# Dense attention of a two-layer decoder: side work moved to other places within a head's time, rows fetched every second head

## The chip, the cores and the metric

One core of a Trainium2 chip runs the whole program. The metric is the device time of one execution in microseconds. The kernel is timed several times; the median stands for it. One further execution is profiled, and that one has its own time.

## The reference, cut to what matters

Two layers: latent attention, a cross attention and a mixture of experts, then dense attention, a sigmoid mix and a quantised feed-forward. The change touches the dense attention stage and the side work done under it. In the reference's terms:

```python
# end of the first layer: x gets the four weighted expert rows of each token
routed = zeros_like(x).at[tok].add(out_slots * flat_w[order][:, None])
x = x + ...                                   # residual, then the next layer
# dense attention (2 batches of 512 in one pass over 8 pairs of heads, twice)
q, k, v = einsum('bpd,hde->bphe', layernorm(x), W_Q / W_K / W_V) + b
attn = softmax(where(causal, q @ k / sqrt(128), IGNORE))
x = x + einsum('bqhe,hed->bqd', attn @ v, W_O) + b_O
# mix with a sigmoid of the context, per token and channel
x = x + 0.6 * sigmoid(si + sj + b) + 0.4 * layernorm(x)
# ternary weights of the feed-forward
scale = 1 / mean(abs(w));  wq = clip(round(w * scale), -1, 1) / scale
```

The token stream `X` has 16 tiles of 128 tokens by 512. Batches 0 and 1 are tiles 0 to 7, batches 2 and 3 are tiles 8 to 15.

## The kernel before, in words

The dense stage is one loop over 64 **slots**, `for i in range(NI + 2)`, written out once per engine. A slot computes the scores and the softmax of head turn i, transposes the probabilities of turn i-1 and multiplies them with V, and projects Q, K and V of turn i+1. In an odd slot the output projection of the last pair of heads comes on top. `DenseOrder.steps(i)` (L1559) gives the order within a slot, and all engines follow it: scores 0 and 1, project Q, transpose 0, project K, scores 2, transpose 1, scores 3, transpose 2, project V, in odd slots four outputs, and then the values. Engines run in order and meet at semaphores.

In this text a time "at 7.84" counts from the start of its slot on PE (the first L1761 matmul of score 0). All matmuls are done in three parts (high and low halves of both operands), so each drained PSUM bank is read twice: ACT copies the high part, and DVE then subtracts to get the low part. For one slot that gives a chain between PE, ACT and DVE:

- Q projection: ACT `d_qk` L1884, DVE `d_qk` L2019, then DVE `d_rv` L2035 (reciprocals for rows 0 and 1 of the softmax); POOL L2217 scales those two rows of P.
- transpose 0: ACT `d_PTh` L1899, DVE `d_PTl` L2042.
- K projection: ACT L1884, DVE L2019. Then DVE `d_mx` L2027 and `d_nb` L2029 of score 2, ACT exponential L1892, ACT L1899 and DVE L2042 of transpose 1, DVE L2027 of score 3, ACT L1892, ACT L1899 and DVE L2042 of transpose 2. The values on PE (L1805 to L1807) wait for that last L2042.
- V projection: ACT `d_Vh` L1878, DVE `d_Vl` L2013. In an odd slot the four outputs are then added to X by DVE, L2048; PE's third output waits for the first of these additions.
- values: ACT `d_zh` L1906, DVE `d_zl` L2053, at the start of the next slot.

In every fourth slot (i = 2, 6, 10, ...; called **splitting slots** here, all of them even) the next pair's weights are split: ACT L1859 after each of the three projections, and POOL L2191, a subtraction of two SBUF tiles: two of them follow POOL's first two L2217, the third follows its last two. SP loads weights one slot after (L1608, L1613).

The **side work** before the change:

- *Additions of later tiles.* Tiles 8 to 15 still lack their four expert rows. POOL fetches the rows with indirect DMAs into `d_cmb` (`fetch`, L2179, four a tile), one tile a slot in slots 18 to 25. DVE adds one tile a slot in slots 20 to 27 (`combine`, L1985): row 0 after project Q, row 1 after project K, row 2 after transpose 1, row 3 after transpose 2, and statistics (`stats`) after project V.
- *Weight sums.* 24 pieces of 128x1024 are loaded by SP into three buffers; ACT sums their absolute values (`absum`, L1910), two a slot in slots 33 to 44, after project Q and project V.
- *Rounding.* In slots 47 to 58 the 24 pieces are loaded again; DVE scales and clips each (`rounded`, L2073 and L2075), after project Q and project V; ACT subtracts a constant and writes bf16 (`settle`, L1916), after project K and project V; SP stores it.
- *Mixing.* Tiles 0 to 7 get the sigmoid mix: DVE takes statistics again (`retake`, after project V in slots 32 to 39), POOL turns them into factors (`weigh`, slots 35 and 39), DVE scales the tile (L2062, after transpose 1 in slot 36+t), ACT computes the tanh (`lean`, L1928, after transpose 2) and DVE adds it (L2066, after project Q of the next slot).

Of the kernel before, what the change touches and what calls it, by code (L numbers as in the profile page):

```python
# [1508 lines left out]
NPC = 24  # L1509


class DenseOrder:
# [22 lines left out]
    def tiles(self, i):  # L1535

        return {0: ((), (4, 5, 6, 7)), 29: ((8,), (9,)), 30: ((10,), (11,)), 31: ((12,), (13,)), 32: ((14,), (15,))}.get(i, ((), ()))

    def sums(self, i):

        return [2 * (i - 33), 2 * (i - 33) + 1] if 33 <= i < 45 else []

    def rounds(self, i):

        return [2 * (i - 47), 2 * (i - 47) + 1] if 47 <= i < 59 else []

    def mixed(self, i):

        return i - 36 if 36 <= i < 44 else -1

    def side(self, i):

# [41 lines left out]
DENSE = DenseOrder()  # L1594
# [78 lines left out]
def dense_sp(e, S, a, M, W, G, wscr):  # L1673
    def weights(ws):
        e.wait_ge(S["d_wl"], 3 * ws)
        dense_load(e, a, W, G, ws)

    def weights_o(ws):
        e.wait_ge(S["d_wol"], ws)
        dense_load_o(e, a, W, G, ws)  # L1680

    def piece(m):
        n = m % NPC
        if 3 <= m < NPC + 3:
            e.wait_ge(S["d_abs"], m - 2)
        elif m >= NPC + 3:
            e.wait_ge(S["d_set"], n - 2)
        dst = M.piece[m % 3] if n < 16 else M.piece[m % 3].rearrange("p (k n) -> p k n", k=2)
        e.dma_start(dst, dense_piece(a, n)).then_inc(S[f"d_pc{m % 3}"], 16)

    def store(n):
        e.wait_ge(S["d_set"], n + 1)
        e.dma_start(wscr[n // 8, :, n % 8 * 1024:n % 8 * 1024 + 1024], M.tern[n % 2]).then_inc(S[f"d_st{n % 2}"], 16)

    for ws in range(1, 8):
        weights(ws)
        weights_o(ws)
    weights(8)
    e.dma_start(M.wi[:, :], a["wiT"]).then_inc(S["d_ctx"], 16)
    e.dma_start(M.bb[:, :], a["L1_xattn_b"].partition_broadcast(128)).then_inc(S["d_ctx"], 16)  # L1700
    e.wait_ge(S["d_cb"], 16)
    e.dma_start(M.cT[:, :, :], a["ctxT"][0:2].rearrange("b p n -> p b n")).then_inc(S["d_ctx"], 16)
    for m in range(3):
        piece(m)
    for i in range(30, 62):
        if i % 4 == 3:
            if i < 56:
                weights((i + 5) // 4)
            weights_o((i + 1) // 4)
        for n in DENSE.sums(i):  # L1710
            piece(n + 3)
        for n in DENSE.rounds(i):
            store(n)
            if n + 3 < NPC:
                piece(NPC + n + 3)
    for r in range(2):
        e.wait_ge(S[f"d_st{r}"], 16 * (NPC // 2))
# [133 lines left out]
def dense_act(e, S, M, W, G):  # L1851
    ps, O = G.ps, DENSE
# [55 lines left out]
    def absum(n):  # L1908
        e.wait_ge(S[f"d_pc{n % 3}"], 16 * (n // 3 + 1))
        e.activation(M.piece[n % 3], M.piece[n % 3], ACT.Abs, accum_out=M.ws[:, n // 8, n % 8:n % 8 + 1]).then_inc(S["d_abs"], 1)  # L1910

    def settle(n):
        e.wait_ge(S["d_rnd"], n + 1)
        if n >= 2:
            e.wait_ge(S[f"d_st{n % 2}"], 16 * (n // 2))
        e.activation(M.tern[n % 2], M.piece[n % 3], ACT.Copy, bias=-MAGIC).then_inc(S["d_set"], 1)  # L1916
# [7 lines left out]
    def lean(t):  # L1924
        e.wait_ge(S["d_b7"], 2 + t // 4)
        if t:
            e.wait_ge(S["d_mixed"], t)
        e.activation(M.sg, M.row, ACT.Tanh, bias=M.si[:, t:t + 1], scale=0.5).then_inc(S["d_sg"], 1)  # L1928
# [12 lines left out]
    for i in range(NI + 2):  # L1941
        if i % 4 == 2 and 6 <= i < NI:
            split_o((i - 2) // 4)
        for s in O.steps(i):
            if s[0] == "s":
                soft(i, s[1])
            elif s[0] == "p":
                project(s[1], s[2])
                if i % 4 == 2 and i + 2 < NI:
                    split_w((i + 2) // 4, "qkv".index(s[1]))  # L1950
                if s[1] in "qv" and O.sums(i):
                    absum(O.sums(i)[s[1] == "v"])
                if s[1] in "kv" and O.rounds(i):
                    settle(O.rounds(i)[s[1] == "v"])
            elif s[0] == "x":
                turn_x(s[1])
            elif s[0] == "b":
                if s[1] in ("m0", "m1"):
                    row(int(s[1][1]))
            elif s[0] == "t":  # L1960
                turn_p(i - 1, s[1])
                if s[1] == 2 and O.mixed(i) >= 0:
                    lean(O.mixed(i))
            elif s[0] == "z":
                values(i - 1)


def dense_dve(e, S, M, W, G):
# [22 lines left out]
    def stats(t):  # L1991
        e.wait_ge(S["d_cb"], t + 1)
        ln_stats_dve(e, S, dv, G, range(t, t + 1))
# [61 lines left out]
    def retake(t):  # L2055
        e.wait_ge(S["d_xa"], 60 if t < 4 else 64)
        ln_stats_dve(e, S, dv, G, range(t, t + 1))
# [53 lines left out]
    combine(5)  # L2111
    project("k", 0)
    for i in range(NI + 2):
        adding = i - 12 if 20 <= i < 28 else -1
        for s in O.steps(i):
            if s[0] == "s":
                peak(i, s[1])
            elif s[0] == "p":
                project(s[1], s[2])
                if s[1] == "q":  # L2120
                    invert(i, 0)
                    invert(i, 1)
                    if 29 <= i <= 32:
                        norm(2 * i - 50)
                        norm(2 * i - 49)
                if adding >= 0:
                    if s[1] == "v":
                        stats(adding)
                    else:
                        combine(adding, ("qk".index(s[1]),))  # L2130
                if s[1] == "q" and O.mixed(i - 1) >= 0:
                    mix(O.mixed(i - 1), 1)
                if s[1] == "q" and i == 45:
                    e.wait_ge(S["d_abs"], NPC)
                    e.tensor_reduce(G.wsc[:, :, 0], M.ws[:, :, :], AX.X, ALU.add).then_inc(S["d_wsum"], 1)
                if s[1] == "v" and 32 <= i < 40:
                    retake(i - 32)
                if s[1] in "qv" and O.rounds(i):
                    rounded(O.rounds(i)[s[1] == "v"])
                if i == 0 and s[1] == "q":  # L2140
                    stats(5)
                if i == 0 and s[1] == "k":
                    combine(7)
            elif s[0] == "x":
                turn_x(s[1])
                if i == 0 and s[1] < 6:
                    norm(s[1] + 2)
            elif s[0] == "b":
                side(s[1])
            elif s[0] == "t":  # L2150
                turn_p(i - 1, s[1])
                if s[1] == 1 and O.mixed(i) >= 0:
                    mix(O.mixed(i), 0)
                if adding >= 0 and s[1] >= 1:
                    combine(adding, (s[1] + 1,))
            elif s[0] == "o":
                output(s[1], s[2])
            else:
                values(i - 1)
            if i == 0 and s == ("s", 1):  # L2160
                stats(4)
                combine(6)
            if i == 0 and s == ("s", 3):
                for t in (6, 7):
                    stats(t)
                norm(4)
                norm(5)
            if i < NI and s == (("t", 2) if i else ("s", 3)):
                if i + 1 == NI:
                    invert(i, 0)  # L2170
                    invert(i, 1)
                invert(i, 2)
                invert(i, 3)


def dense_pool(e, S, M, W, G, eoscr):
# [52 lines left out]
    for i in range(NI):  # L2229
        if i % 4 == 2 and i >= 6:  # L2230
            split_o((i - 2) // 4)
        norm(i, 0)
        norm(i, 1)
        if i == 0:
            for t in (5, 6, 7):
                rstd(t)
        if i % 4 == 2 and i + 2 < NI:
            split_w((i + 2) // 4, 0)
            split_w((i + 2) // 4, 1)
        norm(i, 2)  # L2240
        norm(i, 3)
        if i % 4 == 2 and i + 2 < NI:
            split_w((i + 2) // 4, 2)
        if i < 2:
            for t in range(4 * i, 4 * i + 4):
                bias(t)
        if 18 <= i < 26:
            fetch(i - 10)
        if i == 27:
            ln_rstd_pool(e, S, G, range(8, 12), 12)  # L2250
        if i == 28:
            ln_rstd_pool(e, S, G, range(12, 16), 16)
        if 29 <= i <= 32:
            bias(2 * i - 50)
            bias(2 * i - 49)
        if i in (35, 39):
            weigh((i - 35) // 4)
# [567 lines left out]
```

## Time and profile before

| what | value |
|---|---|
| median of 3 runs | 3533.98 us (3522.2 to 3544.41) |
| profiled execution, its time | 3511.81 us |
| its span, first to last instruction | 3510.5 us |
| mean granted TensorE clock | 0.955 |
| busy: PE, DVE, ACT, POOL | 89%, 55%, 44%, 38% of the span |
| chain that ended last: PE, DVE, ACT, issue | 56%, 16%, 7%, 6% of the span |
| dense stage loop | about 1945 to 3108 us of the span |

A window row of the trace gives the length of a stretch, each engine's busy time with its number of instructions, and the mean granted TensorE clock (1.00 is the upper level). A timeline row gives start, duration, engine, line, operation, output<-inputs, and in brackets how long the engine sat idle before it and who released it. Starts and ends of neighbours overlap by up to 0.1 us, because instructions are pipelined. PE is busy 89% on average, but the stage has quiet slots and disturbed ones, and only the rows by slot show the difference.

### The profile page before, as it was taken

How to read it: one execution, taken by the hardware profiler on the slowest of the kernel's cores; microseconds unless marked ns; L12 is line 12 of the kernel's file. 1: busy time of each engine (PE TensorE's matmuls, PEld its weight loads, DVE VectorE, ACT ScalarE, POOL GpSimd, SP SyncE). 2: the span in 40 equal slices, each digit the busy share in tenths (PEclk: the TensorE clock that was granted, in tenths of full speed). 3: DMA queues.
4: the chain of work that ended last, by engine and by line, in shares of the span. 5: the costliest groups of instructions: out<-in, count | busy, mean ns of one | idle time of the engine just before them, and what ended most of it. 6: DMA issues, size and time to landing. Idle time of an engine off the chain costs nothing.

```text
span 3510.5 us, 47291 instructions
## 1 busy us (share of the span) xinstructions
PE 3135.9 (89%) x17554; PEld 2141.0 (61%) x17587; DVE 1935.9 (55%) x3349; ACT 1541.3 (44%) x2738; POOL 1349.2 (38%) x1271
## 2 busy tenths in 40 slices
PE   7899886899897789999995899988999999988898
PEld 3344432433333458888884788877887877855565
DVE  3454444677775634444444544455555556557776
ACT  1222221577776324444442344433455544435554
POOL 2324232333321655665664533454434444310000
PEclk9899898799998899999997899999999999999999
DMA  3000000000002125665665101122022233020000
GB/s 116 1 1 1 1 1 7 6 1 1 1 1 71 37 88 189 198 201 189 199 199 164 49 25 30 49 78 85 25 85 79 85 109 109 30 78 7 13 13 19
DMA packets 148007, 231.56 MB, mean 66 GB/s; under 512 B 12314, under 2 KB 70511, under 8 KB 147524
## 3 DMA queue, kind: packets, MB, share of 16 engines
q1 hardware_dynamic: 130372, 178.15, 15.7%
q0 software_dynamic: 17408, 50.38, 4.9%
q8 instruction: 142, 2.33, 0.3%
q14 instruction: 85, 0.70, 0.1%
HBM read 180.16 MB, written 48.33 MB: 65 GB/s over the span
## 4 chain that ended last, share of the span: by engine, by line
PE 56%; DVE 16%; ACT 7%; issue 6%; POOL 1%; DMA 1%; SPq 0%; POOLq 0%; ACTq 0%; DVEq 0%; another core or an unknown queue 0%
PE ps L1370 10%; PE ps L1372 9%; PE ps L1371 9%; PE ps L829 3%; PE ps L840 3%; PE ps L797 2%; PE ps L2395 2%; DVE d_PTl L2042 2%; DVE d_mx L2027 2%; PE ps L1090 2%; PE ps L2425 2%; PE ps L2414 1%; ACT d_PTh L1899 1%; DVE d_qk L2019 1%; ACT d_qk L1884 1%
## 5 line engine op out<-in xcount | busy, mean ns | idle before, releaser
L2217 POOL TENSOR_SCALAR d_P<-d_P,d_rv 128x128 f32<-128x128 f32 (+3 forms) x256 | 302.2, 1191 | 548.6 <-DVE d_rv L2035 548.3
L937 DVE TENSOR_REDUCE b_mx<-ps 128x2 f32<-128x1024 f32 x256 | 312.4, 1224 | 115.9 <-PE ps L818 114.1
L904 ACT ACTIVATE b_PT<-ps 128x512 f32<-128x512 f32 x512 | 278.5, 600 | 62.3 <-PE ps L829 58.2
L1492 POOL TENSOR_TENSOR x_wl<-x_wr,x_wh 128x1024 fp32r<-128x1024 f32 x96 | 227.5, 2401 | 185.6 <-ACT x_wh L1416 185.5
L1892 ACT ACTIVATE d_P<-ps,d_nb 128x128 f32<-128x128 f32 (+3 forms) x256 | 135.1, 528 | 253.4 <-DVE d_nb L2029 249.4
L829 PE MATMUL ps<-b_Q,b_KT 64*128 64x512 f32 x512 | 208.3, 469 | 19.6 <-ACT b_PT L904 19.5
L1370 PE MATMUL ps<-d_xh,d_wh 128*128 128x512 f32 x512 | 215.7, 421 | 1.4 <-DVE d_xl L2004 1.4
L818 PE MATMUL ps<-b_KT,b_Q 64*128 64x512 f32 x512 | 205.1, 482 | 4.0 <-DVE b_mx L937 3.1
L1372 PE MATMUL ps<-d_xh,d_wl 128*128 128x512 f32 x512 | 204.1, 399 | 0.0
L2042 DVE TENSOR_TENSOR d_PTl<-ps,d_PTh 128x384 fp32r<-128x384 f32 (+1 forms) x192 | 114.9, 599 | 159.7 <-ACT d_PTh L1899 159.3
L1371 PE MATMUL ps<-d_xl,d_wh 128*128 128x512 f32 x512 | 202.2, 395 | 0.0
L1370 PE MATMUL ps<-x_XH,x_wh 128*128 128x512 f32 x512 | 199.6, 390 | 1.4 <-DVE x_XL L1456 1.4
L1372 PE MATMUL ps<-x_XH,x_wl 128*128 128x512 f32 x512 | 199.7, 390 | 0.0
L1371 PE MATMUL ps<-x_XL,x_wh 128*128 128x512 f32 x512 | 199.5, 390 | 0.0
L462 ACT ACTIVATE a_P<-ps 128x2048 f32<-128x2048 f32 (+1 forms) x48 | 76.4, 1593 | 215.8 <-PE ps L326 194.3
L1464 DVE TENSOR_TENSOR x_ag<-ps,x_sg 128x512 f32<-128x512 f32 x64 | 44.3, 692 | 217.0 <-PE ps L1372 217.0
L1483 POOL DMA_INDIRECT x_Xe<-hscr,x_TI x128 | 139.7, 1092 | 59.1 <-issue 29.7
L829 PEld LDWEIGHTS ps<-b_Q,b_KT 64*128 64x128 f32 x512 | 84.6, 187 | 124.7 <-ACT b_PT L904 88.4
L1370 PE MATMUL ps<-d_wh,d_xh 128*128 128x256 f32 x512 | 151.1, 295 | 1.4 <-DVE d_xl L2004 1.4
L1370 PE MATMUL ps<-d_woh,d_zh 128*128 128x512 f32 x256 | 110.0, 430 | 41.7 <-DVE X L2048 37.0
L1372 PE MATMUL ps<-d_wh,d_xl 128*128 128x256 f32 x512 | 145.8, 285 | 0.0
L1371 PE MATMUL ps<-d_wl,d_xh 128*128 128x256 f32 x512 | 145.8, 285 | 0.0
(378 smaller groups left out, 8383.9 us busy)
## 6 DMA issues: line engine op xcount, KB each, us to landing
x_wr<-in_L_ffn_w SPq DMA_DIRECT2D x32, 1024.0 KB, 7.9
eoscr<-x_eo SPq DMA_DIRECT2D x32, 1024.0 KB, 5.4
x_wr<-in_L_ffn_w SPq DMA_DIRECT2D x32, 512.0 KB, 8.6
d_w<-in_L_attn_W_Q SPq DMA_DIRECT2D x32, 256.0 KB, 3.3
d_w<-in_L_attn_W_K SPq DMA_DIRECT2D x32, 256.0 KB, 4.5
d_w<-in_L_attn_W_V SPq DMA_DIRECT2D x32, 256.0 KB, 5.3
d_wo<-in_L_attn_W_O SPq DMA_DIRECT2D x16, 512.0 KB, 5.6
d_cmb<-in_wgT SPq DMA_DIRECT2D x16, 512.0 KB, 3.9
```

The lines of the kernel that those rows point to most:

```text
L818: e.matmul(ps[:, 2 * (t % 2) + h, :], M.Q1[rows, r % 4, q * 128:q * 128 + 128], M.KT[rows, b % 2, g, :], start=True, stop=True).then_inc(S ...
L829: e.matmul(ps[:, 4 + y, :], M.KT[rows, b % 2, g, k * 128:k * 128 + 128], M.Q2[rows, (2 * j + p) % 4, :], start=True, stop=True).then_inc(S ...
L904: e.activation(M.PT[:, half, v % 2, 2 * p + y, :], ps[:, 4 + y, :], ACT.Exp, scale=0.25).then_inc(S["b_ex"], 1)
L937: e.tensor_reduce(M.mx[:, r % 2, q, :], ps[:, 2 * (t % 2):2 * (t % 2) + 2, :], AX.X, ALU.max).then_inc(S["b_mx"], 1)
L1370: e.matmul(out, lh, rh, start=j == 0, stop=False)
L1371: e.matmul(out, lh, rl, start=False, stop=False)
L1372: t = e.matmul(out, ll, rh, start=False, stop=j == n - 1)
L1483: e.indirect_dma_start(out=M.Xe[:, z, s, :], out_offset=None, in_=hscr, in_offset=bass.IndirectOffsetOnAxis(ap=W.TI[:, 4 * x + s:4 * x + s ...
L1492: e.tensor_tensor(M.wl[:, z, k:k + 2, :], W.wr[:, z, k:k + 2, :], M.wh[:, z, k:k + 2, :].bitcast(F32), ALU.subtract).then_inc(S["x_wl"], 1)
L1892: e.activation(M.P[:, y, POFF[q]:POFF[q] + w], ps[:, q % 2, 0:w], ACT.Exp, bias=M.nb[:, y, q:q + 1], scale=SCALE, accum_out=M.sm[:, y, q:q ...
L2042: e.tensor_tensor(M.PTl[:, c0:c0 + n], ps[:, 2 + c % 2, 0:n], M.PTh[:, c0:c0 + n].bitcast(F32), ALU.subtract).then_inc(S["d_tl"], 1)
L2217: e.tensor_scalar(P, P, M.rv[:, y, q:q + 1], None, ALU.mult).then_inc(S["d_nm"], 1)
```

## The change

It moves the side work; nothing is computed differently. Positions are those of `steps(i)`.

- Additions: tiles 8 to 15 are added in slots 12 to 27, one tile in two slots: rows 0 and 1 after transpose 0 of the even slot, row 2 after transpose 0 of the odd slot, row 3 and the statistics after the last output. Fetches are issued in slots 10, 12, ..., 24.
- Sums and rounding: `pieces(i, first)` gives three pieces to an odd slot and one to an even slot. `absum`: one after transpose 0, in odd slots two more after project V. `rounded`: one after transpose 0, in odd slots two more after the last output. `settle`: one after project V, in even slots two more (those rounded after the outputs) after transpose 0. SP's order of loads and stores stays as it was.
- Mixing: one slot later (slots 37 to 45). DVE's addition and the next tile's scaling stand together after transpose 0, the tanh after project K, and two `retake` after the last output of slots 33, 35, 37 and 39.

```diff
+    def pieces(self, i, first):
+        n = 2 * (i - first)
+        if not 0 <= n < NPC:
+            return [], []
+        return ([n], [n + 1, n + 2]) if i % 2 else ([n + 1], [])
+
     def sums(self, i):
-        return [2 * (i - 33), 2 * (i - 33) + 1] if 33 <= i < 45 else []
+        return self.pieces(i, 33)
     def rounds(self, i):
-        return [2 * (i - 47), 2 * (i - 47) + 1] if 47 <= i < 59 else []
+        return self.pieces(i, 47)
     def mixed(self, i):
-        return i - 36 if 36 <= i < 44 else -1
+        return i - 37 if 37 <= i < 45 else -1
+    def added(self, i):
+        return 8 + (i - 12) // 2 if 12 <= i < 28 else -1
...
 # dense_act
-                if s[1] in "qv" and O.sums(i):
-                    absum(O.sums(i)[s[1] == "v"])
-                if s[1] in "kv" and O.rounds(i):
-                    settle(O.rounds(i)[s[1] == "v"])
+                if s[1] == "k" and O.mixed(i) >= 0:
+                    lean(O.mixed(i))
+                if s[1] == "v":
+                    for n in O.sums(i)[1]:
+                        absum(n)
+                    for n in O.rounds(i)[0]:
+                        settle(n)
...
                 turn_p(i - 1, s[1])
-                if s[1] == 2 and O.mixed(i) >= 0:
-                    lean(O.mixed(i))
+                if s[1] == 0:
+                    for n in O.sums(i)[0]:
+                        absum(n)
+                    for n in O.rounds(i - 1)[1]:
+                        settle(n)
...
 # dense_dve
-        adding = i - 12 if 20 <= i < 28 else -1
...
-                if adding >= 0:
-                    if s[1] == "v":
-                        stats(adding)
-                    else:
-                        combine(adding, ("qk".index(s[1]),))
-                if s[1] == "q" and O.mixed(i - 1) >= 0:
-                    mix(O.mixed(i - 1), 1)
...
-                if s[1] == "v" and 32 <= i < 40:
-                    retake(i - 32)
-                if s[1] in "qv" and O.rounds(i):
-                    rounded(O.rounds(i)[s[1] == "v"])
...
                 turn_p(i - 1, s[1])
-                if s[1] == 1 and O.mixed(i) >= 0:
-                    mix(O.mixed(i), 0)
-                if adding >= 0 and s[1] >= 1:
-                    combine(adding, (s[1] + 1,))
+                if s[1] == 0:
+                    if O.added(i) >= 0:
+                        combine(O.added(i), (2,) if i % 2 else (0, 1))
+                    if O.mixed(i - 1) >= 0:
+                        mix(O.mixed(i - 1), 1)
+                    if O.mixed(i) >= 0:
+                        mix(O.mixed(i), 0)
+                    for n in O.rounds(i)[0]:
+                        rounded(n)
             elif s[0] == "o":
                 output(s[1], s[2])
+                if s[2] == 3:
+                    if O.added(i) >= 0:
+                        combine(O.added(i), (3,))
+                        stats(O.added(i))
+                    if 33 <= i < 40:
+                        retake(i - 33)
+                        retake(i - 32)
+                    for n in O.rounds(i)[1]:
+                        rounded(n)
...
 # dense_pool, after the slot's own work
-        if 18 <= i < 26:
-            fetch(i - 10)
+        if 10 <= i < 26 and i % 2 == 0:
+            fetch((i + 6) // 2)
```

## Rows read from the trace of the kernel before

**Rows 1.** Windows: quiet even slot 10, odd slot 11; slots 20-27; 33-43; 47-58.

```profile
2118.79:2133.15 14.36, 14.02 (x89) 11.95 (x87) 7.12 (x19) 10.05 (x19) 9.39 (x6) 1.00 0.13 37
2133.15:2152.78 19.63, 19.50 (x112) 16.44 (x111) 9.68 (x23) 6.27 (x15) 8.75 (x7) 1.00 0.29 81
2288.82:2453.46 164.64, 143.23 (x786) 119.89 (x785) 97.65 (x224) 57.76 (x128) 82.53 (x67) 0.94 0.27 82
2540.81:2745.58 204.77, 192.03 (x1112) 162.19 (x1111) 113.54 (x275) 108.58 (x231) 86.97 (x70) 0.99 0.28 88
2794.24:3018.15 223.91, 207.05 (x1179) 174.23 (x1177) 132.98 (x299) 108.78 (x215) 99.70 (x61) 0.98 0.34 105
```

**Rows 2.** Window of slot 34, with eight small matmuls of the mix on PE.

```profile
2561.48:2577.02 15.54, 15.54 (x104) 13.80 (x103) 8.24 (x22) 11.23 (x22) 9.48 (x6) 1.00 0.11 35
```

**Rows 3.** Timeline of PE in slot 22, which starts at 2329.91: its stall.

```profile
2346.02 0.58 PE L1805 MATMUL ps<-d_PTh,d_Vh 128*128 128x256 f32 x1 [2.44 <-DVE d_PTl L2042]
```

**Rows 4.** Timeline of DVE in quiet slot 16, which starts at 2220.78.

```profile
2221.70 0.75 DVE L2053 SCALAR_TENSOR_TENSOR d_zl<-ps,d_bv,d_zh 128x512 fp32r<-128x512 f32 x1 [1.89 <-ACT d_zh L1906]
...
2228.62 0.75 DVE L2019 SCALAR_TENSOR_TENSOR d_qk<-ps,d_bk,d_qk 128x512 fp32r<-128x512 f32 x1 [1.71 <-ACT d_qk L1884]
```

**Rows 5.** Timeline of ACT in slot 16, and the tile view of `d_cmb`.

```profile
2227.90 0.69 ACT L1884 ACTIVATE d_qk<-ps,d_bk 128x512 fp32r<-128x512 f32 x1 [2.01 <-PE ps L1372]
...
L1916 ACT ACTIVATE d_cmb<-d_cmb x24: 1042/1057/1058, 2801.9 to 3019.6; 128x1024 bf16<-128x1024 f32 x24
...
DMA to landing us min/median/max: 2.0/3.7/8.1
```

**Rows 6.** Timeline of DVE and POOL in quiet splitting slot 14, which starts at 2186.78.

```profile
2194.62 0.75 DVE L2019 SCALAR_TENSOR_TENSOR d_qk<-ps,d_bk,d_qk 128x512 fp32r<-128x512 f32 x1 [1.06 <-ACT d_qk L1884]
...
2192.35 1.50 POOL L2217 TENSOR_SCALAR d_P<-d_P,d_rv 128x128 f32<-128x128 f32 x2 [1.22 <-DVE d_rv L2035]
2193.82 4.79 POOL L2191 TENSOR_TENSOR d_wl<-d_w,d_wh 128x1024 fp32r<-128x1024 f32 x2
```

**Rows 7.** Timeline of DVE and POOL in slot 22, the splitting slot with additions.

```profile
2335.36 0.73 DVE L1985 SCALAR_TENSOR_TENSOR X<-d_cmb,Wt,X 128x512 f32<-128x512 f32 x1
2338.41 1.99 DVE L1985 SCALAR_TENSOR_TENSOR X<-d_cmb,Wt,X 128x512 f32<-128x512 f32 x1
...
2337.44 5.24 POOL L2191 TENSOR_TENSOR d_wl<-d_w,d_wh 128x1024 fp32r<-128x1024 f32 x2
```

**Rows 8.** Timeline of DVE and POOL in splitting slot 38; L2062's line view.

```profile
2639.73 0.67 DVE L2066 SCALAR_TENSOR_TENSOR X<-d_xn,X 128x512 f32<-128x512 f32 x1
2645.11 1.70 DVE L2062 TENSOR_SCALAR X<-X,d_ab 128x512 f32<-128x512 f32 x1
...
2641.74 4.79 POOL L2191 TENSOR_TENSOR d_wl<-d_w,d_wh 128x1024 fp32r<-128x1024 f32 x2
...
L2062 DVE TENSOR_SCALAR X<-X,d_ab x8: 536/537/1711, 2608.6 to 2735.8; 128x512 f32<-128x512 f32 x8
```

**Rows 9.** Timeline of DVE in slot 49: one piece rounded after project V.

```profile
2844.88 0.74 DVE L2073 TENSOR_SCALAR d_cmb<-d_cmb,wsc 128x1024 f32<-128x1024 f32 x1
2845.66 0.87 DVE L2075 TENSOR_SCALAR d_cmb<-d_cmb 128x1024 f32<-128x1024 f32 x1
```

**Rows 10.** Timeline of DVE and POOL in slot 21: an addition beside POOL's L2217.

```profile
2313.00 0.84 DVE L1985 SCALAR_TENSOR_TENSOR X<-d_cmb,Wt,X 128x512 f32<-128x512 f32 x1
...
2312.22 1.51 POOL L2217 TENSOR_SCALAR d_P<-d_P,d_rv 128x128 f32<-128x128 f32 x2
```

**Rows 11.** Windows of slots 21, 22, 26 and 49: clock and PE time.

```profile
2304.49:2329.91 25.42, 22.18 (x112) 18.37 (x111) 14.67 (x34) 6.27 (x15) 14.80 (x14) 0.87 0.29 82
2329.91:2347.47 17.56, 14.91 (x88) 12.50 (x87) 11.03 (x24) 10.06 (x19) 10.30 (x6) 0.94 0.11 32
2412.29:2429.21 16.92, 14.28 (x89) 11.87 (x87) 10.40 (x23) 10.06 (x19) 9.67 (x6) 1.00 0.17 47
2829.79:2853.48 23.69, 21.25 (x112) 17.66 (x111) 13.81 (x29) 9.23 (x18) 8.82 (x6) 0.93 0.32 100
```

More of the change, by code:

```diff
@@ L1709, in dense_sp @@
             weights_o((i + 1) // 4)
-        for n in DENSE.sums(i):
+        for n in sum(DENSE.sums(i), []):
             piece(n + 3)
-        for n in DENSE.rounds(i):
+        for n in sum(DENSE.rounds(i), []):
             store(n)
```

## The prediction, made before the changed kernel was run

> **What bounds the kernel now.** I read the windows slot by slot first, because PE's 89% hides two kinds of slot. A quiet even slot takes 14.36 us with 14.02 of PE work, a quiet odd one 19.63 with 19.50 [rows 1]: PE sets the pace and nothing moved elsewhere can shorten them. The three stretches with side work are longer. A quiet pair is 33.99. Slots 20 to 27 take 164.64, against 4 x 33.99 = 135.96: 28.7 too much. Slots 33 to 43 (six odd, five even, 189.58 when quiet) take 204.77: 15.2 too much. Slots 47 to 58 take 223.91 against 203.94: 20.0 too much. Together **63.8 us**, the most this change can give back.
>
> Then the waits. In slot 22 PE stands 2.44 us before the values, for DVE's L2042 of transpose 2 [rows 3]. That instruction ends a chain that begins with the K projection: DVE L2019, peak, exponential, transposes 1 and 2, each waiting for the other engine. Whatever is queued on DVE after project K, transpose 1 or transpose 2 lengthens it one for one. Before DVE's L2019 of K there is a hole: after transpose 0 DVE idles 1.71 us [rows 4], ACT 2.01 [rows 5]. Another is at the end of an odd slot, 1.89 before L2053 [rows 4]. In a splitting slot ACT's weight split delays transpose 0, and DVE's hole is 1.06 [rows 6].
>
> A delay costs PE speed as well. PE's busy time in slot 22 is 14.91 instead of 14.02 at a mean clock of 0.94, in slot 49 21.25 instead of 19.50 at 0.93, while slot 26 keeps 1.00 [rows 1, 11]. So a stall of this size sometimes drops the clock to its lower level of 1.2 GHz for a while, at about 1.75 us a time.
>
> **The change part by part.** *Additions.* One row takes 0.73 [rows 7], the next starts 0.05 later because it waits for it. In slots 12, 16, 20, 24 two rows start near 6.1 and end near 7.6; L2019 is due at 7.84: nothing, covered by the 1.71 hole. In odd slots one row fits there. Row 3 and the statistics (0.73 and about 1.1, the latter an estimate from a row of the same width and two tiny instructions) just fill the 1.89. So outside the splitting slots the 28.7 us disappear. The cover gone, a row would cost its 0.75.
>
> In splitting slots 14, 18, 22, 26 DVE is free at 6.78. Row 0 runs to 7.43. POOL's two L2217 end at 5.57 + 1.50 = 7.07 and the weight subtraction L2191 is due at 7.04 [rows 6]. Row 1 can only issue at 7.47. What happens to it is in slot 22: a row that started 0.97 us after L2191 took 1.99 instead of 0.73, and ended 0.56 after the first L2191's 2.40 (half of 4.79) were over [rows 6, 7]. The pair took 5.24 instead of 4.79, so POOL waited in turn. I take it so here: L2191 gets in when row 0 is through (7.3), ends at 9.7, row 1 ends at 10.3, L2019 starts at 10.2 instead of 7.84. Cost 2.3 a slot, 9.2 in all. Bounds: no collision, rows end at 8.25, 0.4 a slot; both halves of the split in front, 4.8.
>
> *Fetches.* They stay at four a tile, now behind POOL's last L2217 of even slots; in splitting slots also behind the third L2191. POOL's first two L2217 of the next odd slot then run later, but PE needs only all four, and the last two wait for reciprocals at the slot's end: nothing. The landing takes 3.7 us, 8.1 at most [rows 5]; a tile's buffer was freed at the end of the odd slot before, and some 15 us are left until its rows are due. The wait of `fetch` is met when reached.
>
> *Sums.* ACT's pieces (1.06 us by the like-sized L1916 [rows 5]) fit in the 2.01 hole after transpose 0, and two after project V in odd slots lie before the outputs, where ACT has nothing to do. Zero; in slots 34, 38, 42 as now, the same instructions in another order between Q's and K's L1884.
>
> *Mixing.* In quiet slots addition (0.67) and scaling (0.54) end near 7.3 [rows 8]: zero. Two `retake` need 2.1 of 1.89; L2053 slips 0.2, which the softmax of scores 0 and 1 absorbs. In slots 38 and 42 the scaling L2062 comes after L2066, at 7.3, when L2191 has begun. Slot 38 shows the price: 1.70 instead of 0.54, ending 0.28 after the pair of L2191 [rows 8]. Now it is the first of the two: end at 10.0, L2019 at 9.9, 2.0 a slot, 4.0 in all; at best 0, at worst 4.5. The small matmuls of slot 34 stay, 15.54 - 14.36 = 1.2 [rows 1, 2]; slots 36 and 40 have fewer, I take 0.5 each (between 0 and 1.2). 2.2 in all.
>
> *Rounding.* L2073 and L2075 take 0.74 and up to 0.87 [rows 9]: 6.05 to 7.7, before 7.84, in all odd slots and in 48, 52, 56: zero, with 0.1 to spare. Two pieces after the outputs take 3.1 of 1.89: L2053 slips 0.9 to 1.2, ACT's Q drain perhaps 0.1. In slots 50, 54, 58 L2075 waits for L2073 and meets L2191 as row 1 does, 0.1 later: 2.4 a slot, 7.2 in all. If it did not collide, ACT would decide: weight split and two `settle` (2 x 1.0) before K's L1884, which starts 0.85 late. At worst 4.9. The `settle` after project V then waits for L2075, and ACT's L1906 of the next slot slips; ACT has slack there. SP's order is unchanged; stores and reloads have a slot's time or most of one, against 8.1 for the longest landing [rows 5].
>
> *Clock.* Nine stalls of 2.0 to 2.4 more. One of the two alike (slots 22, 26) came with a low clock [rows 11]; I take half, 9 x 0.5 x 1.75 = 7.9, with 0 and 15.8 as bounds.
>
> Sum: 9.2 + 4.0 + 7.2 + 2.2 + 7.9 = 30.5 left of 63.8, **gain 33.3**. The profiled execution's 3511.8 becomes 3478.5. The median of the runs is 22 us above it; I take the gain from it: 3534.0 - 33.3 = **3501**.
>
> Beside a collision there is a weaker contact: in slot 21 an addition started while POOL's second L2217 ran and took 0.84, not 0.73, and ended only 0.11 after it [rows 10]. I price such contacts at 0.1, inside the slack. The Trainium skill, SBUF — State Buffer, section "Who interferes with whom", says that a DVE instruction with two SBUF inputs, or in a two-port mode, and a GpSimd one that reads SBUF take the shared port pair in turn, whoever starts first for its whole instruction. For L2191 the trace agrees (1.99 for 0.73). For L2217 it does not (0.84); by the rule that row would have waited to the end of L2217.
>
> **Rivals.** (a) *The later DVE instruction gets in ahead of the split.* Against it: it issues 0.4 us after L2191 is due; for it: L2062 has no wait before it and follows L2066 directly. Left over: 4 x 0.4 + 3 x 0.85 + 2.2 = 6.4; gain 57.4, 3477.
>
> (b) *Waits of whole instructions also for L2217.* The first DVE instruction in the hole would wait for POOL's first L2217 (to about 6.3), the second for the next; L2019 comes 0.6 late in the 13 quiet slots with two instructions (four of additions, nine of rounding): 8 more, gain 25, 3509. Rows 10 speak against it. This is the rule that the Trainium skill's page states, worked out here from rows.
>
> (c) *Slower: the DVE instruction waits behind both L2191*, in slots 14 to 58 with splits, until 12.1; L2019 is 4.8 late (4.5 in slots 38 and 42), 42.6 in nine slots. Stalls that long go with a clock like slot 21's, 22.18 of PE instead of 19.50 [rows 1, 11], 2.7 each, 24.1. With 2.2 that leaves 69, 5 more than now: 3539. It decides from 61.6 / 9 = 6.8 us a slot. Against it: in slot 22 the row got in between the two L2191 [rows 7].
>
> (d) *A transfer comes late*, a fetched tile or a reloaded piece: it decides from 15 us of landing, against 8.1; 15 us lost over the stage give 3516.
>
> **Chances.** Forecast 0.60, (a) 0.20, (b) 0.08, (c) 0.05, (d) 0.07. The forecast's own range, by the clock's bounds, is 3493 to 3509. With (a) below and (b) and the runs' scatter of 11 above, the range is 3470 to 3520. One per cent, 35 us, is about what a measurement can tell: (a) lies beyond it, and some four tenths of the forecast, where few stalls cost clock. Faster by over 1%: 0.46; within: 0.50; slower: 0.04.
>
> **What would show it.** In the changed profile: slots 12, 13, 16, 17, 47 to 49 at 14.36 and 19.63; L1985 as 0.74 and about 2.8 in slots 14, 18, 22, 26; L2062 at 2.7 in slots 38 and 42; L2075 at 2.8 in 50, 54, 58; these slots at 16.4 to 16.8; no PE wait for L2048. Wrong if they stay at 14.8 (a), if slot 12 exceeds 14.5 (b), or if splitting slots pass 18 (c).

## The result

| | before | changed |
|---|---|---|
| median of 9 runs | 3526.28 us (3522.20 to 3544.41) | 3501.99 us (3494.24 to 3517.16) |
| ratio | | 0.9928, interval 0.9908 to 0.9947 |
| span of the profiled execution | 3510.5 us | 3515.8 us |
| slot 0 starts | 1944.6 us | 1974.0 us |
| slot 0 to slot 63 | 1141.6 us | 1114.6 us |

The kernel became 0.7% faster: 25 us, between 19 and 32 by the interval. The forecast was 33 us and 3501 us. That the median met the number to a microsecond is partly luck: with more runs the median of before was 3526, not 3534. The ratio of the forecast, 0.9906, lies just outside the interval.

The profiled execution of the changed kernel is *longer* than that of before. That is nothing the change did: its slot 0 starts 29.5 us later, after stages in which both kernels have the same instructions. The loop that was changed is 27.0 us shorter. A single span can't be compared here, a stretch can.

This is the window view of the changed kernel, as in [rows 1]: quiet slots 12 and 13, splitting slot 14, splitting slot 18 and slot 19 behind it; then slots 20 to 27, 33 to 43, 47 to 58, and 12 to 19. The columns are length, busy time with count of PE, PEld, DVE, ACT and POOL, clock, DMA share, GB/s.

```profile
2182.36:2196.72 14.36, 14.01 (x89) 11.94 (x87) 8.52 (x21) 6.29 (x15) 2.71 (x3) 1.00 0.00 1
2196.72:2216.36 19.64, 19.50 (x113) 16.43 (x111) 11.31 (x26) 6.28 (x15) 10.29 (x10) 1.00 0.20 54
2216.36:2233.06 16.70, 14.28 (x89) 11.86 (x87) 11.24 (x24) 10.07 (x19) 10.12 (x6) 1.00 0.10 32
2286.76:2303.79 17.03, 14.60 (x88) 12.19 (x87) 11.24 (x24) 10.07 (x19) 10.44 (x6) 0.98 0.09 32
2303.79:2324.66 20.87, 20.73 (x111) 17.44 (x111) 11.27 (x26) 6.28 (x15) 12.33 (x11) 0.94 0.42 126
2324.66:2468.46 143.80, 137.71 (x787) 116.11 (x785) 86.16 (x197) 57.82 (x128) 69.13 (x53) 0.98 0.18 52
2555.84:2754.48 198.64, 193.61 (x1113) 163.39 (x1111) 113.54 (x273) 109.77 (x232) 87.37 (x70) 0.98 0.29 93
2803.13:3018.40 215.27, 205.59 (x1178) 173.28 (x1177) 140.49 (x300) 108.33 (x216) 91.23 (x62) 0.98 0.36 109
2182.36:2324.66 142.30, 136.20 (x786) 114.64 (x785) 85.45 (x194) 57.84 (x128) 71.60 (x56) 0.99 0.20 60
```

Slots 12 and 13 carry additions and are as short as quiet ones: 14.36 and 19.64. The three stretches went from 164.6, 204.8 and 223.9 [rows 1] to 143.8, 198.6 and 215.3. Slots 12 to 19, quiet before, take 142.3 instead of 136.0, and slot 59 2.3 more. Apart from the mix's small matmuls (slots 34, 36 and 40), what is left stands in nine splitting slots and right behind them. Slot 19 holds no PE work that a quiet odd slot has not, yet PE is busy for 20.73 instead of 19.50, at a clock of 0.94. A fall of the clock shows mostly in the odd slot behind the stall: slots 38 and 42 have a mean of 1.00 themselves, slots 39 and 43 have 0.92.

The timeline of DVE and then POOL in slot 14, which answers [rows 6, 7]; the slot starts at 2216.36:

```profile
2222.44 0.69 DVE L2059 TENSOR_TENSOR d_PTl<-ps,d_PTh 128x512 fp32r<-128x512 f32 x1 [0.55 <-ACT d_PTh L1910]
2223.05 3.58 DVE L2002 SCALAR_TENSOR_TENSOR X<-d_cmb,Wt,X 128x512 f32<-128x512 f32 x2
2226.55 0.74 DVE L2036 SCALAR_TENSOR_TENSOR d_qk<-ps,d_bk,d_qk 128x512 fp32r<-128x512 f32 x1
...
2221.93 1.51 POOL L2236 TENSOR_SCALAR d_P<-d_P,d_rv 128x128 f32<-128x128 f32 x2 [1.22 <-DVE d_rv L2052]
2223.41 5.51 POOL L2210 TENSOR_TENSOR d_wl<-d_w,d_wh 128x1024 fp32r<-128x1024 f32 x2
```

Two additions take 3.58 us together, where two alone take 1.5. The K drain L2036 starts at 10.19 of the slot instead of 7.84: 2.35 late, and the rest of the chain with it. POOL's two subtractions take 5.51 instead of 4.79: 2.68 and 2.89, where each alone takes 2.41.

The timeline of DVE in slots 38 and 50, which answers [rows 8, 9]; they start at 2644.99 and 2856.85:

```profile
2651.68 0.68 DVE L2083 SCALAR_TENSOR_TENSOR X<-d_xn,X 128x512 f32<-128x512 f32 x1
2652.28 2.65 DVE L2079 TENSOR_SCALAR X<-X,d_ab 128x512 f32<-128x512 f32 x1
2654.85 0.74 DVE L2036 SCALAR_TENSOR_TENSOR d_qk<-ps,d_bk,d_qk 128x512 fp32r<-128x512 f32 x1
...
2863.55 0.93 DVE L2090 TENSOR_SCALAR d_cmb<-d_cmb,wsc 128x1024 f32<-128x1024 f32 x1
2864.51 2.80 DVE L2092 TENSOR_SCALAR d_cmb<-d_cmb 128x1024 f32<-128x1024 f32 x1
2867.23 0.74 DVE L2036 SCALAR_TENSOR_TENSOR d_qk<-ps,d_bk,d_qk 128x512 fp32r<-128x512 f32 x1
```

The scaling takes 2.65 instead of 0.54, the second half of the rounding 2.80 instead of 0.74; K's drain starts 2.02 and 2.54 late. The forecast had 2.7 and 2.8 for these two, and 2.0 and 2.4 for the delays.

And PE in slot 18, which answers [rows 3]: the stall is in two parts, since transposes 1 and 2 are both late.

```profile
2300.08 0.44 PE L1816 MATMUL ps<-d_PTh,d_Vh 128*128 128x384 f32 x1 [0.65 <-DVE d_PTl L2059]
2302.65 0.39 PE L1816 MATMUL ps<-d_PTh,d_Vh 128*128 128x256 f32 x1 [1.78 <-DVE d_PTl L2059]
```

### The profile page after: what moved, and what is told of

It reads as the page before. It is cut to its first block, busy times and chain, and to the rows that moved or that the text cites. A ratio compares the mean times of both kernels' runs of the same rounds, so it can differ in the third digit from the quotient of the medians.

```text
span 3515.8 us, 47291 instructions
## 1 busy us (share of the span) xinstructions
PE 3165.6 (90%) x17554; PEld 2158.5 (61%) x17587; DVE 1947.3 (55%) x3349; ACT 1542.3 (44%) x2738; POOL 1342.8 (38%) x1271
## 4 chain that ended last, share of the span: by engine, by line
PE 56%; DVE 16%; ACT 6%; issue 6%; DMA 1%; POOL 1%; another core or an unknown queue 0%; DVEq 0%; ACTq 0%; SPq 0%; POOLq 0%
PE ps L1370 9%; PE ps L1372 9%; PE ps L1371 9%; PE ps L829 3%; PE ps L840 3%; PE ps L797 2%; PE ps L2414 2%; DVE d_PTl L2059 2%; DVE d_mx L2044 2%; PE ps L1090 2%; PE ps L2433 2%; PE ps L2444 2%; ACT d_PTh L1910 1%; DVE d_qk L2036 1%; PE ps L1816 1%
## 5 line engine op out<-in xcount | busy, mean ns | idle before, releaser
L2236 POOL TENSOR_SCALAR d_P<-d_P,d_rv 128x128 f32<-128x128 f32 (+3 forms) x256 | 290.3, 1146 | 525.6 <-DVE d_rv L2052 525.2
L660 POOL TENSOR_TENSOR a_acc<-a_P 128x1536 f32<-128x1536 f32 x16 | 54.8, 3426 | 234.5 <-ACT a_P L462 234.5
```

The source lines that it names most:

```text
L2236: e.tensor_scalar(P, P, M.rv[:, y, q:q + 1], None, ALU.mult).then_inc(S["d_nm"], 1)
```

## Experiments

Three things were open: is it really POOL's instruction that holds DVE, how much of what is left comes from the clock, and does each part bring what the trace says. A ratio compares with the kernel before as it was timed beside that run: a median of 3517.7 us for e1, e2 and e3, 3530.5 us for e6. "Loop" is slot 0 to slot 63 in one profiled execution.

**e1_front.** Only DVE's order in splitting slots is changed: the same work ahead of transpose 0, when POOL's subtraction isn't due yet.

```diff
+    def beside(i):
+        if O.added(i) >= 0:
+            combine(O.added(i), (2,) if i % 2 else (0, 1))
+        if O.mixed(i - 1) >= 0:
+            mix(O.mixed(i - 1), 1)
+        if O.mixed(i) >= 0:
+            mix(O.mixed(i), 0)
+        for n in O.rounds(i)[0]:
+            rounded(n)
...
+                if s[1] == "q" and i % 4 == 2:
+                    beside(i)
...
-                if s[1] == 0:
-                    if O.added(i) >= 0:
-                        combine(O.added(i), (2,) if i % 2 else (0, 1))
...
+                if s[1] == 0 and i % 4 != 2:
+                    beside(i)
```

> The changed kernel, but in splitting slots (i = 2, 6, 10, ...) DVE's side work stands after project Q and the two reciprocals, ahead of transpose 0, instead of behind it; ACT's is unchanged. Theory P (DVE's second instruction waits for POOL's weight subtraction): issued near 5.45 and 6.22 both are over at 6.96, before the subtraction is due at 7.04. No DVE side instruction over 1.0 us; slots 14, 18, 22, 26, 38, 42 at 14.4 to 14.5; slots 50, 54, 58 at 15.2, because two settle and the weight split on ACT make K's drain 0.85 late; no slot behind them over 20.0, since the low clock came from the stalls. Stage loop from slot 0 to slot 63 about 1083 us (before 1141.6, changed kernel 1114.6); ratio 0.983. Rival L (the splitting slots simply hold too much DVE work, wherever it stands): they stay above 16. Rival K (the low clock has another cause, such as load): slots 19, 23, 27, 39, 43 stay above 20.3.

Measured: 3456.4 us, ratio 0.9819 (0.9796 to 0.9843); loop 1083.0. Slots 14, 18, 22, 26, 38 and 42 take 14.36, slots 50, 54, 58 15.07, and no slot behind them more than 19.7. Timeline of DVE and POOL in slot 14 (from 2187.60):

```profile
2193.05 1.52 DVE L2002 SCALAR_TENSOR_TENSOR X<-d_cmb,Wt,X 128x512 f32<-128x512 f32 x2
2194.49 0.69 DVE L2059 TENSOR_TENSOR d_PTl<-ps,d_PTh 128x512 fp32r<-128x512 f32 x1
2195.44 0.75 DVE L2036 SCALAR_TENSOR_TENSOR d_qk<-ps,d_bk,d_qk 128x512 fp32r<-128x512 f32 x1 [0.27 <-ACT d_qk L1895]
...
2193.17 2.19 POOL L2241 TENSOR_SCALAR d_P<-d_P,d_rv 128x128 f32<-128x128 f32 x2 [1.23 <-DVE d_rv L2052]
2195.33 4.80 POOL L2215 TENSOR_TENSOR d_wl<-d_w,d_wh 128x1024 fp32r<-128x1024 f32 x2
```

The same work in the same slot costs nothing: the two additions take 1.52, and K's drain is on time at 7.84. Rivals L and K fall. Now POOL pays: its L2241 take 2.19 instead of 1.50, with nobody waiting.

**e2_best.** The same, and ACT's second `settle` of a splitting slot moves to the hole before score 3.

```diff
-                    for n in O.rounds(i - 1)[1]:
+                    for n in O.rounds(i - 1)[1][:1 if i % 4 == 2 else 2]:
                         settle(n)
+                if s[1] == 1 and i % 4 == 2:
+                    for n in O.rounds(i - 1)[1][1:]:
+                        settle(n)
```

> As e1_front, and in splitting slots ACT does one of the two settle after transpose 0 and the other after transpose 1, where it waits 1.4 us for DVE anyway. Theory P: slots 50, 54, 58 fall from 15.2 to 14.4 to 14.6; stage loop about 1080 us; ratio 0.982, the side matmuls of the mix (2.2 us) being all that is left of the 63.8. Rival L: as before above 16. If e1_front already has 50, 54, 58 at 14.4, my reading of ACT's queue was wrong and this run equals e1_front.

Measured: 3456.7 us, ratio 0.9814 (0.9793 to 0.9836); loop 1079.8. Slots 50, 54 and 58 fall from 15.07 to 14.36 to 14.38, so ACT's queue was read rightly: two `settle` made K's drain late by 0.7. The 2.1 us can't be seen in the ratios, whose intervals overlap; and of the 3.2 by which the loop is shorter than in e1_front, 1.4 stand in slots 0 and 1, which the edit doesn't touch. This version leaves 2.0 us of the 63.8, the mix's small matmuls, and beats both kernels: 1.9% below before.

**e3_halves.** POOL's subtraction is issued as two half ones; nothing is moved.

```diff
-        e.tensor_tensor(M.wl[:, j, :, :], W.w[:, j, :, :], M.wh[:, j, :, :].bitcast(F32), ALU.subtract).then_inc(S["d_wl"], 1)
+        e.tensor_tensor(M.wl[:, j, 0:2, :], W.w[:, j, 0:2, :], M.wh[:, j, 0:2, :].bitcast(F32), ALU.subtract).then_inc(S["d_half"], 1)
+        e.tensor_tensor(M.wl[:, j, 2:4, :], W.w[:, j, 2:4, :], M.wh[:, j, 2:4, :].bitcast(F32), ALU.subtract).then_inc(S["d_wl"], 1)
```

> The changed kernel, with each of POOL's weight subtractions (128x1024) issued as two of 128x512, nothing moved. Theory P (DVE waits for the POOL instruction that runs, whole): the second addition of a splitting slot takes about 1.6 instead of 2.8, the slots are 15.3 to 15.6 instead of 16.4 to 17.5, the stall on PE is 1.0 to 1.3 and the low clock behind it appears in fewer than three of nine. Ratio about 0.986. Rival W (DVE waits until POOL has nothing more to do, or for the weights as a whole): second addition still 2.8 or more, slots as in the changed kernel. Rival F (it has nothing to do with POOL): same as the changed kernel, too.

Measured: 3466.0 us, ratio 0.9848 (0.9826 to 0.9871); loop 1094.0. Slots 14 to 26 take 15.6, 38 and 42 15.3, the others 15.8; only slot 59 behind them is long (21.24). Tile view of `d_cmb` (minimum, median, maximum in ns), and timeline of POOL in slot 14:

```profile
L2002 DVE SCALAR_TENSOR_TENSOR X<-d_cmb,Wt,X x48: 741/752/1681, 1916.3 to 2439.5; 128x512 f32<-128x512 f32 x48
...
2204.56 1.55 POOL L2210 TENSOR_TENSOR d_wl<-d_w,d_wh 128x512 fp32r<-128x512 f32 x1
2206.07 1.77 POOL L2211 TENSOR_TENSOR d_wl<-d_w,d_wh 128x512 fp32r<-128x512 f32 x1
```

In the changed kernel the longest addition took 2.80, here 1.68: 1.12 less, and half a subtraction is 1.1 shorter than a whole one (1.30 and 2.41). DVE waits for the POOL instruction that runs, and gets in before the next, which is then longer by about 0.5 (1.77 for 1.30). PE's stalls in the nine slots are 1.25 to 1.75, somewhat longer than expected, and the clock fell behind one of them. Rivals W and F fall.

**e6_late.** DVE's order is that of the change; POOL waits with its subtractions instead.

```diff
         if i % 4 == 2 and i + 2 < NI:
+            e.wait_ge(S["d_pl"], O.index["k", i + 1] + 1)
             split_w((i + 2) // 4, 0)
```

> The changed kernel, with one wait more: in splitting slots POOL's first weight subtraction waits until DVE has drained K. DVE's order is that of the change. Theory P: nothing runs on POOL beside DVE's side work, so the second addition takes 0.74, slots 14, 18, 22, 26 are 14.8 (the 0.4 of rival (a)), 38 and 42 14.4 to 14.5, 50, 54, 58 15.2; POOL's two subtractions end near 13.4, before the last two rows of P are due at 13.7. Stage loop about 1085 us, ratio 0.984. Rival Q (POOL has no room left: its scaling of P comes late and PE waits at transpose 0 of the next slot): slots 15, 19, ... above 20.5, ratio 0.99 or more.

Measured: 3471.5 us, ratio 0.9841 (0.9811 to 0.9871); loop 1086.1. Slots 14 to 26 take 14.65, 38 and 42 14.36, the others 15.08. Both additions together take 1.53. The three stretches keep 6.9 us over quiet slots, 1.55 of them the exception that follows. So rival (a)'s price of 6.4 was about 1 us too high (0.3 and 0.7 a slot instead of 0.4 and 0.85); its condition does not hold in the changed kernel. Rival Q falls. One thing I had not expected is slot 34, 17.09 instead of 15.54. Timeline of DVE and POOL there:

```profile
2555.09 2.38 DVE L2103 COPY d_wj<-d_wi 128x128 f32<-128x128 f32 x1 [0.21 <-PE ps L1827]
...
2554.97 4.80 POOL L2210 TENSOR_TENSOR d_wl<-d_w,d_wh 128x1024 fp32r<-128x1024 f32 x2 [1.59 <-DVE d_qk L2036]
```

The late subtraction now meets a small DVE copy, which waits for it in the same way: 2.38 us for 128 columns. In the kernel before the same copy met the last 0.65 of a subtraction and took 0.73.

**e4_add_only, e7_mix_only, e8_round_only.** The kernel before with one part of the change each; the other two parts stand where they stood. For e4 that is this, besides the fetches:

```diff
-        adding = i - 12 if 20 <= i < 28 else -1
...
-                if adding >= 0:
-                    if s[1] == "v":
-                        stats(adding)
-                    else:
-                        combine(adding, ("qk".index(s[1]),))
...
-                if adding >= 0 and s[1] >= 1:
-                    combine(adding, (s[1] + 1,))
+                if s[1] == 0:
+                    if O.added(i) >= 0:
+                        combine(O.added(i), (2,) if i % 2 else (0, 1))
...
+                if s[2] == 3:
+                    if O.added(i) >= 0:
+                        combine(O.added(i), (3,))
+                        stats(O.added(i))
```

> The kernel before, with only the additions and fetches of the change. By the forecast: slots 20 to 27 lose their 28.7 us; slots 14, 18, 22, 26 are 16.4 to 17.3 and three of the slots behind them 1 us longer at a low clock; from slot 33 on everything as before (204.8 and 223.9). Stage loop about 1141.6 - 28.7 + 9.2 + 4 = 1126. Rival D (spread over 16 slots the additions or fetches disturb quiet slots, too): slots 12, 13, 15, 16, 17 above 14.6 or 19.9.

> The kernel before, with the change's mixing and weight sums alone. Slots 33 to 44 as in the changed kernel: 9.0 us over quiet slots instead of 15.1, so a gain of about 6; additions and rounding stay as before (28.7 and 19.9). Stage loop about 1135.5, give or take a fall of the clock. If the parts help or hinder each other, the three separate gains won't add up to the 27.0 of the whole.

> The kernel before, with the change's rounding alone. Slots 47 to 59 as in the changed kernel: 13.5 us over quiet slots instead of 19.9, a gain of about 6.4; slots 20 to 44 as before. Stage loop about 1135, give or take a fall of the clock. With additions alone (11.3 measured) and mixing alone the sum should come to 24 to 27.

Measured, as the loop's length against 1141.6: additions 1130.3 (11.3 less), mixing and sums 1135.1 (6.5 less), rounding 1135.4 (6.2 less). Together 24.0, against 27.0 for the whole. Counted over quiet slots, each part in its own stretch, the additions bring 13.0 (14.6 in the whole change), mixing and sums 6.3 (6.1), rounding 6.3 (6.4): 25.6 against 27.1. The 1.5 between them are a fall of the clock behind slot 14, which e4 has and the changed kernel has not. The rest lies in slots that the parts do not touch, such as slot 39 of e4 with 24.3 instead of 21.6; e10_before's loop was 1.6 shorter than that of before, so such scatter has that size. e4 missed its 1126 by 4: 2.5 of it in slots 12 to 28, where four falls came instead of three and cost 6.3 instead of 4, and the rest in slots that it shares with the kernel before. The clock fell behind all nine splitting slots with moved side work in these three runs. Rival D falls: slots 12, 13, 16 and 17 are quiet, and slot 15 (21.08) is long only behind splitting slot 14. Each part leaves its trace where the forecast put it, and each gives back less than its stretch had lost.

**e5_ladder.** e2_best, with idle reductions behind K's drain of every fourth slot: late values without POOL.

```diff
+LADDER = ((2, 365), (2, 557), (3, 461), (3, 589), (4, 509))
...
+                if s[1] == "k" and i % 4 == 0 and 4 <= i <= 60:
+                    m, n = LADDER[(i // 4 - 1) % 5]
+                    for z in range(m):
+                        e.tensor_reduce(M.junk[:, 4 * (i // 4) - 4 + z:4 * (i // 4) - 3 + z], G.cst[:, 0:n], AX.X, ALU.max)
```

> e2_best with useless DVE reductions of constants put behind DVE's K drain in slots 4, 8, ..., 60: 1.0, 1.4, 1.8, 2.2, 2.6 us of them in turn, three slots of each. POOL and the side work have no part in it. It measures what a late values step costs by itself, stall and clock. Theory S (the stall alone sets the clock): each slot is longer by the reductions' time, with a stall on PE 0.35 longer than that; after 1.0 and 1.4 the clock stays up, as in e3_halves (stalls of 1.4 to 1.6 us: one fall in nine), after 2.2 and 2.6 it falls in most of six, as in the changed kernel (eight of nine), each fall costing 1.0 to 1.8 us. Rival B (POOL's or ACT's activity or the DMAs of the side work belong to it): the clock stays up in all fifteen slots.

Measured: the five steps lengthen their slots by 0.9, 1.3, 1.6, 2.0 to 2.1 and 2.4 to 2.6 (slots 36 and 40, which take 14.61 without the reductions, by only 1.8 and 2.1). Behind the first three steps, nine slots in all, the clock never fell. Behind the other two it fell in four of six. Windows of slots 4 and 5 (first step), 16 and 17 (fourth), 40 and 41, 60 and 61 (fifth):

```profile
2038.01:2053.24 15.23, 14.00 (x88) 11.93 (x87) 7.89 (x21) 6.28 (x15) 2.20 (x3) 1.00 0.00 1
2053.24:2072.89 19.65, 19.51 (x113) 16.44 (x111) 9.69 (x23) 6.28 (x15) 6.39 (x6) 1.00 0.00 1
2245.82:2262.28 16.46, 14.36 (x88) 11.94 (x87) 11.30 (x27) 6.29 (x15) 2.79 (x3) 0.99 0.00 0
2262.28:2283.39 21.11, 20.96 (x111) 17.64 (x111) 11.28 (x26) 6.28 (x15) 10.68 (x10) 0.92 0.18 51
2673.43:2690.15 16.72, 14.94 (x90) 12.24 (x89) 11.47 (x29) 8.53 (x19) 4.55 (x8) 1.00 0.09 33
2690.15:2709.79 19.64, 19.50 (x112) 16.43 (x111) 10.90 (x25) 10.00 (x22) 6.89 (x6) 1.00 0.24 81
3023.60:3040.32 16.72, 14.28 (x89) 11.86 (x87) 9.38 (x23) 6.28 (x15) 2.22 (x3) 1.00 0.00 0
3040.32:3061.52 21.20, 21.06 (x113) 17.68 (x111) 9.69 (x23) 6.28 (x15) 6.37 (x6) 0.92 0.00 1
```

Slot 61 has no side work and no DMA, and its PE work takes 21.06 instead of 19.50. So the stall by itself is enough, and rival B falls. Theory S holds in kind, with four of six for "most". The two slots in which the clock stayed up are 36 and 40, and there PE did not stand still for as long. Both hold small matmuls of the mix (PE works 14.94 in slot 40 and 14.28 in slot 60), and one of the two parts of the stall is gone. PE's stall in slot 40, and the two in slot 60:

```profile
2689.33 0.38 PE L1818 MATMUL ps<-d_PTh,d_Vh 128*128 128x256 f32 x1 [1.78 <-DVE d_PTl L2064]
...
3036.93 0.44 PE L1818 MATMUL ps<-d_PTh,d_Vh 128*128 128x384 f32 x1 [0.66 <-DVE d_PTl L2064]
3039.50 0.38 PE L1818 MATMUL ps<-d_PTh,d_Vh 128*128 128x256 f32 x1 [1.77 <-DVE d_PTl L2064]
```

By the time that PE stood still, the ladder has no exception: 1.2 to 1.8 us in eleven slots (36 with 1.50 and 40 with 1.78 among them) and no fall, 2.1 to 2.4 us in four slots (16, 20, 56, 60) and four falls. The other runs have few exceptions: stalls of 1.25 to 1.75 in e3_halves gave one fall in nine, and stalls of 2.1 to 2.6 in the changed kernel (twice) and in e4, e7 and e8 gave 25 in 27. What was different in the two stalls without a fall, both in slot 14 with 2.4, is not settled.

**e9_again, e10_before.** The two kernels unchanged, profiled once more.

> The changed kernel itself, profiled once more. Stage loop near 1114.6 again, with the clock low behind seven to nine of the nine splitting slots with side work, if that is a property of stalls of this size. If it is chance, near the half that the forecast took, four or five, and the loop is 1109. The stages ahead of slot 0 have the same instructions in both kernels: slot 0 started at 1944.6 in the kernel before and at 1974.0 in the changed one; if this is scatter of executions, it starts elsewhere this time.

> The kernel before, profiled once more. Stage loop near 1141.6, within 3 us. Start of slot 0 anywhere from 1944 to 1975, if the early stages scatter; at 1944.6 if they don't, and then the changed kernel's 1974.0 would need another reason.

Measured: the changed loop takes 1112.7, with a slow clock behind the same eight of nine splitting slots (not behind slot 14, behind which it did fall in e4); before takes 1140.0. Slot 0 started at 1954.9 and 1953.3, and over all twelve profiles anywhere from 1944.1 to 1974.0. The 29.5 us ahead of the loop are scatter of executions. Windows of slots 18 and 19 of e9_again, which repeat those above:

```profile
2267.40:2284.31 16.91, 14.51 (x89) 12.09 (x88) 11.23 (x24) 10.07 (x19) 10.31 (x6) 0.98 0.09 32
2284.31:2305.25 20.94, 20.81 (x111) 17.55 (x111) 11.27 (x26) 6.27 (x15) 12.42 (x11) 0.93 0.42 126
```

## Why the prediction was right, and where its size was off

The lengths over quiet slots in the changed kernel come to 36.6 us: 14.1 in slots 12 to 28, 9.0 in 33 to 44, 13.5 in 47 to 59. The forecast was 30.5.

- *What could be won, 63.8.* Right. e2_best gives back 61.8 of it.
- *Holes after transpose 0 and at the end of odd slots hide the work.* Right in every slot without a split. The two overruns foreseen (two `retake`, two roundings after the outputs) cost nothing.
- *Collision with POOL's subtraction, 20.4.* Right in place, in order and in size: the K drains start 2.35, 2.02 and 2.54 late, 4 x 2.35 + 2 x 2.02 + 3 x 2.54 = 21.1. Of each 2.54, 0.7 would be left without POOL, by the two `settle` (e1_front's 15.07); the forecast had said so. e1, e3 and e6 show that it is a collision and with what. The forecast's step "row 1 ends 0.56 after the first L2191" came from [rows 7], and that row was enough.
- *The mix's small matmuls, 2.2.* 1.8, the length over quiet slots of e1_front in slots 33 to 44.
- *Clock, 7.9.* This is the term that was mis-sized. What is left, 36.6 - 21.1 - 1.8 = 13.7, is eight falls instead of four and a half. Taken one by one (a splitting slot and the slot behind it over quiet ones, less K's delay) seven cost 1.3 to 1.6 and the one behind slot 58 2.9, 1.7 on average against the 1.75 of the forecast. The price was about right, the share wrong: I took "half" from the two like slots of [rows 11]. Both came right behind a low clock (slots 21 and 25, at 0.87 and 0.93), and in e10_before they changed places: slot 22 at 1.00, slot 26 at 0.93. Two such cases are no basis for a share. In the changed kernel, where quiet slots lie between the stalls, it is eight of nine, twice. The bound of 15.8 held.
- *Loads, fetches, stores, SP.* The trace's list of waits of the changed loop has none for any of them.

With the 36.6 that are left the gain is 63.8 - 36.6 = 27.2, against 27.0 measured in the loop and 25 in the ratio.

Of the rivals, (a) was a fair price for a case that did not come: it takes another order to get it, and e6_late had it. (b), whole-instruction waits for POOL's L2236 as well, is wrong here: slots 12, 16, 20 and 24 are at 14.36 to 14.37. Its contact is seen often and is small: the second instruction in the hole takes 0.85 instead of 0.74 in slots 12, 48 and 49, and L2090 takes 0.93 in slots 50, 54 and 58. That is up to 0.2 where I had allowed 0.1, and still inside the slack. The rule of the Trainium skill (SBUF — State Buffer, "Who interferes with whom"), by which the one that starts first holds the other for its whole instruction, fits POOL's long subtraction of two SBUF tiles: the DVE instruction that came second ended 0.3 to 0.6 after it. For DVE behind L2236 the measurement decides against "the whole instruction". The other way round POOL's scaling did pay for DVE's side work: its second L2236, 0.93 alone, took 1.42 in slot 12 and 1.77 in slot 48. (c) would have needed DVE to miss the gap between two subtractions; it never did. (d) did not happen.

## What to carry to other kernels

A hole in one engine's timeline is only free if no long instruction for which the filling has to wait runs beside it, as POOL's subtraction did here: lay the other engine's long instructions beside the hole before filling it, and count from the moment the *second* instruction can issue. If two such works must share a slot, put the short ones first; here that alone was worth 30 us, more than the whole change. Where a change leaves stalls of over 2 us on PE, add the clock to their price, and compare stretches of a loop rather than spans when the rest of the program scatters by more than the effect.

## What the runs showed of the hardware

- An addition, a scaling, a rounding step or a copy on DVE (inputs in SBUF) that meets a running POOL subtraction of two SBUF tiles waits for what is left of it: 2.80 instead of 0.74 behind one of 128x1024, 1.68 behind one of 128x512, and 2.38 for a copy of 128 columns. POOL's next subtraction is then 0.2 to 0.5 longer (2.61 in slot 38, 2.89 in slot 14, for 2.41).
- Not every DVE instruction waits: the K drain, which reads one of its two tiles from PSUM, took its usual 0.75 in the middle of the subtraction [rows 6].
- POOL's scaling of 128x128 and 128x256 held DVE by 0.2 at most, and was itself up to 0.8 longer beside DVE's side work.
- Where PE stood still for 1.2 to 1.8 us in a slot, the clock fell behind one slot of twenty (e5, e3). Where it stood 2.1 to 2.6 us, it fell behind 29 of 31 (the changed kernel twice, e4, e7, e8, e5). In the changed kernel such a fall cost 1.3 to 1.6 us, and once 2.9.
